# One layer of linear attention and routed experts: the first batch's inputs in pieces on two transfer queues, its normalisation on VectorE, its masks ahead of its inverses

## The reference

```python
xn = (x - mean(x)) / sqrt(var(x) + 1e-5)
# attention: 16 heads of 16 channels
q, k, v = split(xn @ wqkv); q, k = relu(q), relu(k)
num = einsum('bhnd,bhnde->bhne', q, cumsum(k[..., :, None] * v[..., None, :]))
den = einsum('bhnd,bhnd->bhn', q, cumsum(k))[..., None] + 1e-5
attn = merge_heads(num / den) @ wo
# experts: 8 routes, of which 4 are MLPs (256 -> 128 -> 256)
scores = sigmoid(xn @ Wr); idx = top2(scores + router_bias)
cw = scores[idx] / (sum(scores[idx]) + 1e-9)          # zero elsewhere
routed  = sum_e cw[e] * ((silu(xn @ Wg[e]) * (xn @ Wu[e])) @ Wd[e])
routed += (cw[4] + cw[6]) * xn + cw[7] * relu(xn)
shared  = causal depthwise conv of 4 taps over xn + conv_b
out = x + attn + routed + shared
```

## Time and profile before

| what | value |
|---|---|
| median of three runs | 1348.21 us |
| the profiled execution, its own time | 1346.54 us |
| its span in the profile | 1344.8 us |
| PE busy in 50 to 90, 90 to 130, 900 to 940, 1260 to 1300 us | 40.00 us in each |
| VectorE, ScalarE, GpSimd busy, of the span | 83%, 55%, 61% |
| x of batch 0 issued, used | 0.72, 4.28 us |
| wqkv issued, used | 2.22 and 2.73, 9.40 us |
| sizes: x of a batch, tables, wqkv, gate and up, down, wo | 512, 209, 2 x 384, 4 x 256, 512, 256 KB |
| one issue of a DMA on SP | 0.43 to 0.53 us, once 2.81 |

### The profile page before, as it was taken

How to read it: one execution, slowest core, us unless ns; L and a number is a source line. 1 busy time by engine, 2 the same in 40 slices (tenths; PEclk the granted TensorE clock), 3 DMA queues, 4 the chain that set the end, 5 groups by cost and what they waited for, 6 DMA issues and landing times.

```text
span 1344.8 us, 54748 instructions
## 1 busy us (share of the span) xinstructions
PE 1313.8 (98%) x24384; PEld 1136.4 (85%) x24384; DVE 1114.9 (83%) x2566; ACT 738.3 (55%) x1545; POOL 814.9 (61%) x679
## 2 busy tenths in 40 slices
PE   4899999999999999999999999999999999999997
PEld 3788888888888888888888888888888888888886
DVE  4888888888888888988888988888888889888885
ACT  4555665555664565654555655555645656545561
POOL 2755666755666656657556666556566566575554
PEclk9999999999999999999999999999999999999999
DMA  4011111111111211111111111121111111111110
GB/s 148 34 66 65 51 48 34 65 65 66 46 53 34 65 65 64 35 45 55 66 65 51 48 35 65 65 65 42 56 35 66 65 65 35 34 65 50 50 49 18
DMA packets 46779, 73.73 MB, mean 55 GB/s; under 512 B 6480, under 2 KB 42192, under 8 KB 42448
## 3 DMA queue, kind: packets, MB, share of 16 engines
q1 hardware_dynamic: 46544, 70.24, 15.1%
HBM read 53.18 MB, written 17.04 MB: 52 GB/s over the span
## 4 chain that ended last, share of the span: by engine, by line
PE 97%; DVE 1%; SPq 1%; ACT 1%; DMA 1%; issue 0%; DVEq 0%
PE ring L300 51%; PE scores L300 17%; PE ring L408 7%; PE ring L422 6%; PE scores L357 5%; PE state_sum L371 4%; PE ring L440 2%; PE scores L310 2%; PE scores L339 2%; DMA x_t<-in_L_attn_x_dram 1%; SPq L257 0%; DVE cT L775 0%; ACT qp L517 0%; DVE sm L753 0%; ACT xn L528 0%
## 5 line engine op out<-in xcount | busy, mean ns | idle before, releaser
L626 POOL TENSOR_TENSOR hid<-hid,cwb 128x512 f32<-128x512 f32 x128 | 169.8, 1327 | 202.6 <-DVE hid L783 200.8
L775 DVE SCALAR_TENSOR_TENSOR cT<-xT,conv_ws,cT 128x512 f32<-128x512 f32 x192 | 288.8, 1543 | 0.0
L614 POOL TENSOR_TENSOR x_t<-x_t,same 128x1024 f32<-128x1024 f32 x32 | 77.1, 2409 | 264.3 <-ACT same L524 264.3
L540 ACT ACTIVATE sg<-ring 128x512 f32<-128x512 f32 x128 | 76.7, 599 | 281.5 <-PE ring L300 281.5
L300 PE MATMUL ring<-xl,wgu_h 128*128 128x512 f32 x512 | 212.0, 414 | 0.0
L300 PE MATMUL ring<-xh,wgu_l 128*128 128x512 f32 x512 | 202.5, 396 | 0.0
L300 PE MATMUL ring<-xh,wgu_h 128*128 128x512 f32 x512 | 201.8, 394 | 0.0
L630 POOL TENSOR_TENSOR hl<-hid,hh 128x512 fp32r<-128x512 f32 x128 | 193.2, 1509 | 0.0
L783 DVE TENSOR_TENSOR hid<-ring,sg 128x512 f32<-128x512 f32 x128 | 88.2, 689 | 110.9 <-PE ring L300 110.9
L480 ACT ACTIVATE yh<-yT 128x256 fp32r<-128x256 f32 x128 | 53.5, 418 | 228.9 <-DVE yT L796 228.9
L753 DVE TENSOR_TENSOR sm<-scores,causal_s 128x512 f32<-128x512 f32 x256 | 158.7, 681 | 20.4 <-PE scores L357 20.2
(11 more groups left out here) (110 smaller groups left out, 3542.6 us busy)
## 6 DMA issues: line engine op xcount, KB each, us to landing
cwb<-cw_rows SPq DMA_DIRECT2D x32, 1024.0 KB, 4.6
x_t<-in_L_attn_x_dram SPq DMA_DIRECT2D x32, 512.0 KB, 4.4
out_dram<-x_t SPq DMA_DIRECT2D x32, 512.0 KB, 2.9
cw_rows<-cwt SPq DMA_DIRECT2D x128, 2.0 KB, 1.4
sm<-in_L_attn_wqkv_dram SPq DMA_DIRECT2D x2, 384.0 KB, 5.5
sm<-in_L_ffn_Wg_dram SPq DMA_DIRECT2D x2, 256.0 KB, 4.2
sm<-in_L_ffn_Wu_dram SPq DMA_DIRECT2D x2, 256.0 KB, 5.8
cwb<-in_L_ffn_Wd_dram SPq DMA_DIRECT2D x1, 512.0 KB, 4.2
```

The lines of the kernel that those rows point to most:

```text
L614: pool.tensor_tensor(xb, xb, same[:, :, :], ALU.add).then_inc(s_base1, 1)
L626: pool.tensor_tensor(hid[:, e, :], hid[:, e, :], cwb[:, e, :], ALU.mult).then_inc(s_hid, 1)
L775: ins = dve.scalar_tensor_tensor(out=cT[:, c, :], in0=xT[:, j % 2, c, n:n + BT], scalar=conv_ws[:, c, n:n + 1], in1=cT[:, c, :], op0=ALU.m ...
```

## The change

Seven edits, nearly all in the setup:

1. x of batch 0 is loaded in four pieces with a semaphore each. Tables, wqkv and router weights are issued on ScalarE's queue; SP issues only the rest, the small inputs after wo.
2. ScalarE evaluates one sigmoid on a constant at the start. For batch 0 it makes xh straight from PSUM; VectorE copies xT. Each reads one bank at a time, in opposite order.
3. The normalisation and the low parts of x of batch 0 go from GpSimd to VectorE; PE transposes tile by tile (`turn_first`).
4. The low parts of the four late weight groups go from VectorE to GpSimd, with a semaphore of their own (w_late). PE starts V when two groups are split, and K when four are.
5. VectorE's statistics of batch 1 come after the low parts of batch 0, right ahead of the router.
6. For batch 0, VectorE's inverses come after gate_up(0), behind the masks; ScalarE's relu terms come after first_tap.
7. xn has two buffers; GpSimd's `normalise` for the next batch stands at the tail of a batch behind `base` instead of at the head.

```diff
-        xn = sb("xn", [P, T, D])
+        xn = sb("xn", [P, 2, T, D])
@@ sync
-            sp.dma_start(x_t[:, 0], x_v[0]).then_inc(x_in[0], 16)
-            sp.dma_start(tables_s[:, :], tables).then_inc(tables_in, 16)
-            sp.dma_start(st_r, ...)
-            for c in range(C):
-                sp.dma_start(st_qkv[:, c, :], ...)
-            sp.dma_start(conv_ws...); sp.dma_start(conv_bs...); sp.dma_start(bias_s...)
+            for t in range(T):
+                sp.dma_start(x_t[:, 0, t, :], x_v[0][:, t, :]).then_inc(x_tile[t], 16)
...
+            sp.dma_start(conv_ws...); sp.dma_start(conv_bs...); sp.dma_start(bias_s...)   # after wo
...
-                    sp.wait_ge(w_split, N_SPLITS)
+                    sp.wait_ge(w_split, EARLY)
+                    sp.wait_ge(w_late, N_SPLITS - EARLY)
@@ tensor
+            def turn_first():
+                for t in range(T):
+                    pe.wait_ge(s_xn_tile, t + 1) if t < T - 1 else pe.wait_ge(s_xn, 1)
+                    for c in range(C):
+                        ins = nc.tensor.transpose(XB[c][:, t * P:(t + 1) * P], xn[:, 0, t, c * P:(c + 1) * P],
+                                                  ident_s[:, :])
+                        if t == T - 1:
+                            ins.then_inc(s_xtr, 1)
@@ heads, behind V
+                if not k:
+                    pe.wait_ge(w_split, EARLY)
@@
-            for c in range(C):
-                turn_xn(0, 0, 0, c)
-            pe.wait_ge(w_split, EARLY)
+            turn_first()
+            pe.wait_ge(w_split, 2)
             heads(0, 0, 0)
             scores(0, 0, 0, 0)
             state_sum(0, 0, 0, 0)
-            pe.wait_ge(w_split, N_SPLITS)
+            pe.wait_ge(w_late, N_SPLITS - EARLY)
@@ scalar, in a batch
                 first_tap()
+                if s == j == 0:
+                    relu_terms(0, 0, 0)
@@ scalar, setup
+            act.dma_start(tables_s[:, :], tables).then_inc(tables_in, 16)
+            for c in range(C):
+                act.dma_start(st_qkv[:, c, :], wqkv[c * P:(c + 1) * P, :]).then_inc(qkv_in, 16)
+            act.dma_start(st_r, w_router.rearrange("(c p) n -> p c n", p=P)).then_inc(qkv_in, 16)
+            act.wait_ge(set_up, 3)
+            act.activation(idle[:, :], zeros[:, 0:1], ACT.Sigmoid)
+            act.activation(xT[:, 0, :, 0:HALO], zeros...).then_inc(s_halo, 1)
             high_weights(SPLITS[:EARLY])
-            fill_xT(0, 0, 0)
-            high_x(0, 0, 0)
+            for c in range(C):
+                act.wait_ge(s_xtr, c + 1)
+                if c:
+                    act.wait_ge(s_xT, 1)
+                copy(xh[:, 0, c, :], XB[c][:, :]).then_inc(s_xh, 1)
             high_weights(SPLITS[EARLY:])
             act.wait_ge(small_in, 16 * 3)
             heads(0, 0, 0)
+            same_terms(0, 0, 0)
+            denominators(0, 0, 0)
@@ gpsimd, in a batch
-                if not last:
-                    normalise(s, j, 1)
                 weigh(0)
...
                 if not last:
                     base(s, j, 1)
+                if left > 1:
+                    normalise(s, j, 2)
@@ gpsimd, setup
-            normalise(0, 0, 0)
-            for c in range(C):
-                low_x(0, 0, 0, c)
+            inverse_deviation(0, 0, 0)
+            for n in range(EARLY, N_SPLITS):
+                _, _, hi, lo, src = SPLITS[n]
+                pool.wait_ge(w_hi, n + 1)
+                pool.tensor_tensor(lo, src, hi.bitcast(F32), ALU.subtract).then_inc(w_late, 1)
+            normalise(0, 0, 1)
             base(0, 0, 0)
@@ vector, in a batch
                     gate_up(t)
+                    if s == j == t == 0:
+                        inverses(0, 0, 0)
                     attend(t)
@@ vector, setup
             statistics(0, 0, 0)          # now tile by tile, as x_tile[t] arrives
-            statistics(0, 0, 1)
...
-            low_weights(0, N_SPLITS)
-            dve.wait_ge(small_in, 16 * 3)
+            dve.wait_ge(s_rstd, 1)
+            for t in range(T):
+                dve.tensor_scalar(xn[:, 0, t, :], x_t[:, 0, t, :], negm[:, t:t + 1], rstd[:, t:t + 1], ALU.add,
+                                  ALU.mult).then_inc(s_xn_tile if t < T - 1 else s_xn, 1)
+            low_weights(0, 2)
+            for c in (1, 0):
+                dve.wait_ge(s_xtr, C)
+                if c == 0:
+                    dve.wait_ge(s_xh, 1)
+                ins = dve.tensor_scalar(xT[:, 0, c, HALO:HALO + BT], XB[c][:, :], 1.0, None, ALU.mult)
+                ins.then_inc(s_xT, 1)
+            for c in range(C):
+                dve.wait_ge(s_xT, C)
+                dve.wait_ge(s_xh, c + 1)
+                dve.tensor_tensor(xl[:, 0, c, :], xT[...], xh[...].bitcast(F32), ALU.subtract).then_inc(s_xl, 1)
+            low_weights(2, EARLY)
...
+            dve.wait_ge(small_in, 16 * 3)
+            statistics(0, 0, 1)
             router(0, 0, 0)
             key_sums(0, 0, 0)
             products(0, 0, 0)
-            inverses(0, 0, 0)
+            dve.wait_ge(w_late, N_SPLITS - EARLY)
             mask(0, 0, 0, 0)
             blocks(0, 0, 0, 1)
```

More of the change, by code:

```diff
@@ L1 @@
+import itertools
 from contextlib import ExitStack
@@ L73, in layer_kernel @@
         spare = sb("spare", [P, 1])
+        idle = sb("idle", [P, 1])
         x_t = sb("x_t", [P, BPS, T, D])
-        xn = sb("xn", [P, T, D])
+        xn = sb("xn", [P, 2, T, D])
         stats = sb("stats", [P, T, 6])
@@ L158, in layer_kernel @@
         x_in = [sem(f"x_in{j}") for j in range(BPS)]
+        x_tile = [sem(f"x_tile{t}") for t in range(T)]
         stored = sem("stored")
@@ L227, in load_at @@
         def load_at(s, jk):
-            return s * 16 + (jk // BPS + 1) * 16
+            return (s + jk // BPS + (1 if jk % BPS else 0)) * 16
         SPLITS = [(qkv_in, 3, wvr_h[:, :, 0:D], wvr_l[:, :, 0:D], st_qkv[:, :, 2 * D:3 * D])]
@@ L521, in heads, with same_terms, relu_terms, denominators @@
                     copy(ktok[:, :, g, :], KTB[g][:, :].rearrange("p (t n) -> p t n", t=T)).then_inc(s_ktok, 1)
+            def same_terms(s, j, k):
                 act.wait_ge(s_cw, at(s, j, 1, k + 1))
                 for t in range(T):
[L524 removed]
+                    ins = act.activation(same[:, t, :], xn[:, (j + k) % 2, t, :], ACT.Copy, scale=c46[:, t:t + 1])
                 ins.then_inc(s_same, 1)
+            def relu_terms(s, j, k):
                 act.wait_ge(s_same, at(s, j, 1, k + 1))
                 for t in range(T):
[L528 removed]
+                    xr = xn[:, (j + k) % 2, t, :]
+                    ins = act.activation(xr, xr, ACT.Relu, scale=cw[:, NR - 1, t:t + 1])
                 ins.then_inc(s_relu7, 1)
+            def denominators(s, j, k):
                 act.wait_ge(s_den, at(s, j, 1, k + 1))
@@ L667, in _, with own @@
         def _(dve):
-            count = {"setup": 0, "body": 0, "in_body": False}
-            def own(ins, s, j, apart=False):
+            steps = itertools.count(1)
+            def own(ins, apart=False):
                 ins.then_inc(s_own, 1)
-                if not count["in_body"]:
-                    count["setup"] += 1
-                    dve.wait_ge(s_own, count["setup"])
-                else:
-                    count["body"] += 1
-                    dve.wait_ge(s_own, s * (BPS * OWN_BODY) + (j * OWN_BODY + count["body"] + OWN_SETUP))
+                dve.wait_ge(s_own, next(steps))
                 if apart:
@@ L688, in statistics @@
                 for t in range(T):
+                    if not (s or j or k):
+                        dve.wait_ge(x_tile[t], 16)
                     ins = dve.bn_stats(stats[:, t, :], x_t[:, b, t, :])
-                own(ins, s, j, apart=True)
+                own(ins, apart=True)
                 for t in range(T):
                     ins = dve.bn_aggr(mv[:, t, :], stats[:, t, :])
-                own(ins, s, j)
+                own(ins)
                 dve.tensor_scalar(negm[:, :], mv[:, :, 0], -1.0, None, ALU.mult)
@@ L743, in inverses @@
                 dve.wait_ge(s_dene, at(s, j, 1, k + 1))
-                own(dve.reciprocal(rden[:, :, :], dene[:, :, :]), s, j)
+                own(dve.reciprocal(rden[:, :, :], dene[:, :, :]))
                 for g in range(C):
@@ L825, in batch @@
                     dve.tensor_tensor(xb, OB[t][:, 0:D], xb, ALU.add).then_inc(s_out, 1)
-                if left > 1:
-                    assert count["body"] == OWN_BODY, count
             def low_weights(first, stop):
```

67 lines of the change are left out of this document (35 added, 32 removed).

## The result

The changed kernel takes 1359.18 us, median of 6 runs (1357.10 to 1359.88), against 1348.20 us for the kernel before (6 runs, 1345.83 to 1349.07). The ratio is 1.0083, with a 95% interval of 1.0072 to 1.0094: 11 us slower. The prediction said 8.6 us faster, with 0.02 on slower. Its direction was wrong.

The account below looks back on a forecast made before the run. PE was taken as the bound, busy 1313.8 of 1344.8 us, so only its idle time could be won. An earlier start (8.25) plus masks ahead of inverses (0.34) gave 8.6 us off 1348.2: 1339.6 us, range 1337.2 to 1342.0.

Parts of the forecast that it names:

- Batches 1 to 31: Nothing: Later batches: moving normalise to the tail of the batch before keeps GpSimd's order, so no time changes.
- Rival E: Nothing gained, the start being covered elsewhere or steady batches 0.28 us longer each; chance 0.04 together with other surprises.
- Late low parts on GpSimd: hidden: Setup: GpSimd's four late low parts take 7.5 to 11 us but finish before anything needs them.
- the wait gone: First state sum of batch 0: masks ahead of inverses remove PE's wait of 2.17 us there.
- L = 5.3: Start: the last piece of x of batch 0 lands at 5.3 us, with bounds 4.5 and 6.7.
- Rival A: Start: transfers delay each other and land later than taken, leaving 7.2 us off, 1341.0 us; chance 0.22.
- H: Start: PE begins the heads of batch 0 at 12.85 us instead of 21.11, 8.25 us earlier.
- W: Start: tables and wqkv have landed at 8.2 us, with ends 6.1 and 9.6.
- The new wait at the second state sum: Batch 0: inverses now ahead of the second state block make PE wait 1.8 us, leaving 0.34 of 2.17 gained.
- Rival B: Start: PE's first V matmuls reach the higher clock sooner, up to 2 us more, 10.6 off, 1337.6 us; chance 0.15.

Follow-up runs that it names:

- e2: Kernel before with one unused 4-byte buffer allocated ahead of x_t, no instruction changed: 1356.14 us, ratio 1.0058 to the kernel before.
- e8: Kernel before with 32 unused bytes ahead of xh and 32 behind xl, shifting only these two: 1355.92 us, ratio 1.0071.
- e1: Changed kernel with the 4-byte buffer idle allocated last instead of ahead of x_t: 1350.32 us, ratio 1.0011 to the kernel before.
- e4: Changed kernel with GpSimd waiting for VectorE's low parts of wqk and doubled causal mask before its four late low parts: 1350.64 us.
- e5: Changed kernel with both repairs, e1 and e4 together: 1342.41 us, ratio 0.9966 to the kernel before.
- e7: e5 with the inverses of batch 0 behind the second state block instead of ahead of it: 1339.93 us, ratio 0.9947 to the kernel before.
- e6: e5 with ScalarE's four DMA issues moved to SP's queue, right behind the four pieces of x: 1340.77 us, ratio 0.9962 to the kernel before.
- e10: e11 with the four late low parts back on VectorE and its statistics of batch 1 behind the first state block: 1340.32 us, ratio 0.9938.
- e11: e7 with the one transfer queue of e6: 1340.93 us, ratio 0.9942 to the kernel before.
- e3: Kernel before with an unused 4096-byte buffer behind xn, no instruction changed: 1348.55 us, ratio 1.0002 to the kernel before.
- e9: Kernel before with 32 unused bytes ahead of hh and 32 behind hl, shifting only these two: 1349.03 us, ratio 1.0007.

## Why the prediction was wrong, step by step

**"Batches 1 to 31: Nothing" failed, by 8.8 us.** I looked for a change in the order of work and found none. That was right, and it wasn't enough. Rival E even named a price, 0.28 us a batch, but dismissed it as something "for which the order gives no reason". That 0.28 was also measured is chance: it was the forecast gain spread over the batches. The reason is an address. `idle` moves xh and xl, and 72 matmuls a batch that stream them take 2 to 5.5 ns longer each, 6.8 of the 8.8 us. The rest lies in the down and output products, and its cause is open. e2 puts this loss into the kernel before by that buffer alone, e8 by xh and xl alone, and e1 takes it out again. No row of before could have priced it, but that the buffers move could be seen in the list of allocations. It deserved a rival with a chance of its own.

**"Late low parts on GpSimd: hidden" failed, by 8.5 us.** I weighed GpSimd's own length (7.5 us, 11 if VectorE slowed it) and who waits for its results, and there the answer was right: nobody did. I did not ask what the low parts do to VectorE, which is on the path by way of the router, key sums and masks. Its low parts of wqk and causal_s lost 4.4 and 3.2 us to them, and qks 2.0 to GpSimd's first addition of `base`, which had come forward with the rest. Even with GpSimd held back until the mask is done, the two `hot` operations lost 2.0 in e4, where 0.20 us stay at the first state sum. In e5 one more, scoreb, fell beside a low part, and 1.45 stay, where I had the wait gone:

```profile
21.01 1.14 DVE L740 TENSOR_TENSOR scoreb<-score,bias_s 128x32 f32<-128x32 f32 x1 [1.17 <-ACT score L519]
```

**L = 5.3 failed.** x was complete at 7.36, past the upper bound of 6.7, and at 8.21 and 9.35 in e5 and e7. I had given x half the bytes; the other queue took more (917 against 400 KB by 6 us). e6 has the same four pieces at 4.75, with tables and wqkv behind them on one queue. It is not the cutting into four that is slow. Nor was x merely told late: its last packet ended at 6.87, 0.5 us before VectorE began on it, much as in the kernel before (3.81 and 4.28). Rival A was right that one queue delays the other, and too low in the size; wqkv, which it also had late, was not. By the late x alone H came at 15.00 and not 12.85, 2.15 us.

**What held.** From x's landing on, the chain of steps came out as worked: H - L is 15.00 - 7.36 = 7.6, predicted 12.85 - 5.3 = 7.55. The normalisations on VectorE take 1.38 for four, 0.35 each. The transposes take 1.94, W was 7.58 against 8.2, and the waits of 2.3 ahead of the scores and 3.3 in the last batch stayed. The new wait at the second state sum, forecast at 1.8, measured 1.26 in e5, and moving the inverses (e7) takes it away. Rival B did not come: PE still runs its first 17 V matmuls at half pace, 0.22 us from start to start.

**The sum by these terms.** Of the change without its two faults, e5, I had expected 8.6 us and it gave 4.6. By its profile H is 3.0 later than forecast (15.85), the first state sum keeps 1.45, and the second waits 0.5 less: 8.6 - 3.0 - 1.45 + 0.5 = 4.65. The profiled execution itself gained less: its first output comes at 72.00, 3.9 us before that of the kernel before, and its span is 3.0 shorter. Of what is missing, 0.8 lies ahead of the first output, where the granted clock from 30 to 70 us is 0.92, against 0.96 before:

```profile
30.00:70.00 40.00, 37.29 (x689) 31.11 (x674) 34.36 (x79) 23.25 (x50) 24.16 (x18) 0.92 0.10 32
```

So that 4.65 and 4.6 agree is in part luck. The two faults then take 17.4 back, and 4.6 - 17.4 is 12.8 slower by the terms, where 11.0 were measured. The medians of the kernel before, 1346.69 to 1348.65 beside the experiments, spread by as much as the difference. That e7, e10 and e11 stand near the predicted 1339.6 is no merit of the prediction: they are other kernels.

## What to carry to other kernels

When an edit adds or enlarges a buffer, compare the addresses of all buffers behind it, modulo 64, before and after the edit, those that TensorE streams first; put small new buffers last. When work is moved to GpSimd to free VectorE, list VectorE's two-input operations in the same stretch: each may be held until the GpSimd operation ends, and a short one can lose 1 us like a long one. A second DMA queue took rate from the first here, and x, which the path needed first, came 2.6 to 4.6 us later; weigh that against the issue time that it saves.

## What the hardware showed that was not expected

- A matmul of 512 fp32r columns whose moving operand begins 32 bytes past a multiple of 64 in SBUF has a pitch of 0.2334 us instead of 0.2279 when everything is at full clock (e2 and e8 against before and e3), 2.4%. With gate and up the difference is 1.8 ns.
- The down projection's pitch went from 0.1177 to 0.1207 us when only xh and xl moved (e8), and to 0.1194 when hh and hl moved to a multiple of 64 (e9). No cause was found.
- VectorE's two-input operations in SBUF are held by GpSimd's two-input ones to the end of their instruction: 0.22 became 1.23 (e10, e4), and 1.28 became 5.67 for two (e4, changed kernel).
- GpSimd's normalisation, with one tensor read from SBUF, is held by VectorE's scan: 5.05 us for four (e4) instead of 2.17 (before).
- Four 128 KB pieces of x had landed by 4.5 to 4.75 us with all transfers on one queue (e6, e10, e11) and by 7.3 to 9.4 beside a second queue that moved tables and wqkv (changed kernel, e1, e4, e5, e7).
